# Stacking a pair of images' mixed values in 72 rows by small DMAs, one matmul per query tile in place of three masked ones

## Chip, cores and metric

The kernel runs on one core of a Trainium2 chip. The metric is the device time of one execution in microseconds (us); the median of three runs is compared. The kernel has a program for each engine: TensorE (PE; its weight loads are PEld), VectorE (DVE), ScalarE (ACT), GpSimd (POOL) and SyncE (SP), which here only issues DMAs.

## The reference

One layer of a vision tower on 128 images of 12 channels and 224x224 pixels.

```python
pooled = x.reshape(128, 12, 14, 16, 14, 16).sum(axis=(3, 5))        # 196 tokens an image
h = einsum('bcij,ce->bije', pooled, channel_weights)                # 12 -> 192
n = layernorm(h)
q, k = n[:, :64], n[:, 64:]                                         # 64 queries, 132 keys
a = softmax(q @ k.T * 12 ** -0.5 ...) @ k                           # 64 x 192 an image
a = transpose(a, (0, 2, 1)).reshape(b, 64, 192) @ proj_w.T + proj_b
h = h + concat([a, k])
h = h + moe(layernorm(h))       # 8 experts of 192-128-192 in 4 groups, 2 used a token, and a shared one
```

Only the sum over channels carries an image's content, so the kernel keeps tokens as 12 coefficients (times the fixed channel weights) as long as it can. The attention output of an image is, before the transpose, 64 queries by 12 coefficients; the transpose and reshape mix it with proj_w in three parts r = 0, 1, 2. The item "M" computes these mixed values: for each image a matrix of 12 rows (one per coefficient) and 3 x 192 columns. The query rows after attention are then, for the 64 queries i of an image, the sum over r and coefficient c of (centred channel weight of c at column 3i + r) times (mixed value of c and r), plus the token itself.

## The kernel before, in words

The images go in eight groups of 16. For each group there is an attention stage ("items": V, PHT, VHT, S, U, ET, AH, M, H, X, XT, GQ, keyG, G, gate, C) and then a feed-forward stage of 63 steps (seven chunks of tokens by nine experts). The attention stage of the next group is spread over the steps of the current one's feed-forward stage by a plan written out by hand (`PLAN`, lines 77 to 119, the items of each step); tile loads and sums of the pixels of the group after that are placed by `LATE` (line 136; `LATE0`, line 139, for the first group) in the same steps: one tile at steps 4, 6, 8, 10, 12, 13, 16, 19, 22, 25, 29 and so on, 21 tiles of 1792 KB a group through two slots. The items of the first group run ahead of the loop (lines 404, 405), beside the tile work of `LATE0`. In this document the first group is group zero of the code, the last one the eighth; "groups one to six" are those whose attention stage runs inside another's feed-forward stage with tile work beside it (second to seventh), and the last has no tile work beside it.

Each engine walks the same steps in order and waits by semaphores. On TensorE a step is: the first product of the expert (L1218 for queries, L1392 for keys), the second layer of the step before last (`layer2`, L1368 and L1370), the second product, the gate's row spread by L1397, then the plan's items. On VectorE: two elementwise products (L1123, L1133; L1120 for the shared expert), then the items' parts, then the pixel sums (L770, L777). On ScalarE: the SiLU (L732), then the pixel sums (L630), then the items' parts. On SP (`ffn_dma`, L477): at each step first the load that takes the slot of a tile just summed (`load_after`, L448), and at the fourth step of a chunk the stores of the chunk before (`store`, L468). Step 25 holds a load; step 21 holds the four stores of the second query chunk.

The item M (steps 19, 20 for the first eight images, 23, 24 for the other eight; L1290) makes the mixed values of eight images at once; ScalarE copies them to `Msb` (L681): 96 partitions (12 an image), two halves, 3 x 192 columns. The item H (eight of them, H0 to H7, steps 25 to 30, one for each 128 query rows, that is for a pair of images; L1309) adds in one PSUM bank the token part (a bf16 matmul, L1311) and three f32 matmuls (L1313), one for each r, whose moving operand is all 96 partitions of a half and whose stationary operand `CWr` is zero but for the 24 rows of the pair. VectorE then takes the bank's statistics and copies it to `h2q` (L959, L960).

```python
for q in range(3):
    last = mm(ps[:, 0:D], CWr[:, q, i % 4, :], Msb[:, i // 4, D * q:D * q + D],
              start=False, stop=(q == 2))
```

`CWr` is built once at the start: eight small DMAs (L436) put the centred weights in 8 x 12 partitions, and `spread_cwc` (L841) multiplies them eight times by a column mask made by GpSimd (L531 to L535). The small DMAs stand on SP's queue ahead of nine others (L441) and of all tile loads but the first two.

Of the kernel before, what the change touches and what calls it, by code (L numbers as in the profile page):

```python
# [118 lines left out]
}  # L119
A_FIRST = 2  # L120
# [103 lines left out]
def build(nc, x, cw, proj_w, proj_b, gate_w, gate_b, w1, w2, w3, sw1, sw2, sw3, out):  # L224
    ctx = ExitStack()
    with ctx:
# [17 lines left out]
        CWr = sb("CWr", [128, 3, 4, 128])  # L244
# [57 lines left out]
        CWr_src = Msb[0:8 * CH, 0, 0:D]  # L302
# [16 lines left out]
        rmask = gt[0:8 * CH, 0, 0:8]  # L319
# [29 lines left out]
        const_done, prep_full, prep_dve, prep_act = sem("const_done"), sem("prep_full"), sem("prep_dve"), sem("prep_act")  # L349
        cwc_ready, cwx_split, w_split, wx_in, cwx_in = sem("cwc_ready"), sem("cwx_split"), sem("w_split"), sem("wx_in"), sem("cwx_in")  # L350
# [66 lines left out]
        def _(sp):  # L417
# [16 lines left out]
            sp.wait_ge(cwc_ready, 1)  # L434
            for b in range(8):
                sp.dma_start(CWr_src[b * CH:(b + 1) * CH, :], CW14[0:CH, :]).then_inc(cwr_in, 16)  # L436
# [32 lines left out]

            def load_after(g, t):  # L470

                if t + SLOTS < TILES:
                    load(g, t + SLOTS)
                elif g.k is not None or g.off < NG - 1:
                    load(g.plus(1), t + SLOTS - TILES)

            def ffn_dma(g, left):  # L477
                for step in range(STEPS):
                    c, e = divmod(step, EX)
                    for gt_, t in tiles_at(g, step, left):  # L480
                        load_after(gt_, t)
                    if e == 3 and c > 0:
                        store(g, c - 1)
                store(g, NCH - 1)
# [3 lines left out]
            for step in range(A_FIRST, STEPS):  # L488
                for gt_, t in tiles_at(G(None, -1), step):
                    load_after(gt_, t)  # L490
            ffn_dma(G(None, 0), 2)
# [11 lines left out]
        def _(pool):  # L503
# [20 lines left out]
            for c in range(CH):  # L524
# [6 lines left out]
            link(nc.gpsimd.memset(rmask, 1.0))  # L531
            link(nc.gpsimd.affine_select(out=rmask, in_=rmask, compare_op=ALU.is_ge, fill=0.0, base=0,
                                         pattern=[[-CH, 8]], channel_multiplier=1))
            link(nc.gpsimd.affine_select(out=rmask, in_=rmask, compare_op=ALU.is_ge, fill=0.0, base=CH - 1,
                                         pattern=[[CH, 8]], channel_multiplier=-1))  # L535
# [215 lines left out]
        def _(dve):  # L751
# [35 lines left out]
            plink(v.memset(CWr[8 * CH:128, :, :, :], 0.0))  # L787
            plink(v.memset(Msb[8 * CH:128, :, :], 0.0))
# [7 lines left out]
            dve.wait_ge(pb_in, 16)  # L796
            plink(v.tensor_copy(CSP[:, 0, :], CW14[:, :]))
# [43 lines left out]
            def spread_cwc():  # L841

                dve.wait_ge(cwr_in, 16 * 8)
                for b in range(8):
                    plink(v.tensor_scalar(CWr[0:8 * CH, :, b // 2, 64 * (b % 2):64 * (b % 2) + 64],
                                          CWr_src.rearrange("p (i r) -> p r i", r=3), rmask[:, b:b + 1], None, ALU.mult))
                dve.wait_ge(cwx_in, 9 * 16)
                plink(v.memset(SPT[:, :, :, :, :].rearrange("p a b c d -> p (a b c d)"), 0.0))
                plink(v.memset(SPT[0:NQ, 0:GB, 0, 0, CH + 1:UC], 1.0))
# [299 lines left out]
        def _(pe):  # L1149
# [71 lines left out]
            def item(g, kind, i):  # L1221
# [87 lines left out]
                elif kind == "H":  # L1309

                    mm(ps[:, 0:D], UTq[:, 128 * i:128 * i + 128], CWx[:, :], start=True, stop=False)  # L1311
                    for q in range(3):
                        last = mm(ps[:, 0:D], CWr[:, q, i % 4, :], Msb[:, i // 4, D * q:D * q + D],  # L1313
                                  start=False, stop=(q == 2))
# [120 lines left out]
```

## Time and profile before

| | |
|---|---|
| median of 3 runs | 1875.4 us (1872.0 to 1878.65) |
| the profiled execution | 1880.6 us, its span 1878.9 us |
| TensorE busy | 87% of the span |
| VectorE, ScalarE, GpSimd busy | 66%, 48%, 35% |
| mean granted TensorE clock | 0.935 of full speed |
| DMA | 333 MB, 177 GB/s on average |

Everything in the profile is of one execution. Times in the timeline are microseconds from the start of the span. A group of instructions shows how often it ran, its busy time and the mean of one; an f32 matmul appears as two records. "Idle before" names what ended an engine's wait. The DMA rows give the mean busy share of the 16 DMA engines and what they moved.

### The profile page before, as it was taken

What the parts mean: (1) busy time and instruction counts of PE and PEld (TensorE: products, weight loads), DVE (VectorE), ACT (ScalarE), POOL (GpSimd) and SP (SyncE); (2) the same over time, 40 slices, a digit from 0 to 9 for tenths busy, and PEclk for the clock granted to TensorE, in tenths of its full rate; (3) what the DMA queues carried; (4) which work ended last, traced back from release to release, by engine and by line L of the source; (5) the groups of instructions that cost most, each with busy time, mean ns of one, the idle gap of its engine ahead of it and who ended that gap; (6) DMA issues with size and microseconds to landing.
All of it is one profiled execution on the core that took longest, in us unless ns stands there. A gap on an engine that the chain in (4) does not pass through costs nothing.

```text
span 1878.9 us, 31672 instructions
## 1 busy us (share of the span) xinstructions
PE 1634.6 (87%) x9665; PEld 1260.1 (67%) x9798; DVE 1239.9 (66%) x2344; ACT 905.8 (48%) x2999; POOL 657.5 (35%) x739
## 2 busy tenths in 40 slices
PE   1714639999999989998999989998999999999998
PEld 1203528866787667766787667766787678877876
DVE  6855567577666687578566677578666764566365
ACT  2324433656356654656355654656365643443132
POOL 5334326334443435334443335334534332000000
PEclk9955659989999899989999899999999999999999
DMA  8896755546554465555455455556554530000000
GB/s 304 315 352 239 289 219 196 205 165 222 205 204 182 172 222 216 180 200 207 175 205 204 168 215 204 182 198 223 195 205 174 210 131 10 10 18 18 9 19 26
DMA packets 55455, 333.14 MB, mean 177 GB/s; under 512 B 4237, under 2 KB 33666, under 8 KB 33774
## 3 DMA queue, kind: packets, MB, share of 16 engines
q1 hardware_dynamic: 55062, 330.51, 47.6%
q8 instruction: 83, 1.36, 0.3%
q14 instruction: 94, 0.77, 0.1%
q10 hardware_dynamic: 216, 0.50, 0.1%
HBM read 311.10 MB, written 19.27 MB: 176 GB/s over the span
## 4 chain that ended last, share of the span: by engine, by line
PE 69%; DVE 14%; issue 7%; DMA 6%; ACT 2%; POOL 1%; SPq 1%; DVEq 0%; ACTq 0%; another core or an unknown queue 0%; POOLq 0%
PE bank L1370 25%; PE bank L1218 19%; DMA xt<-in_x 6%; PE bank L1392 6%; PE bank L1397 3%; DVE pooled L770 2%; PE bank L1285 2%; DVE ffn L1123 2%; PE bank L1313 2%; DVE ffn L1133 2%; PE bank L1325 2%; PE bank L1274 1%; PE bank L1280 1%; PE bank L1297 1%; PE bank L1290 1%
## 5 line engine op out<-in xcount | busy, mean ns | idle before, releaser
L1370 PE MATMUL bank<-W2T,ffn 128*128 128x192 f32 (+1 forms) x3600 | 692.8, 331 | 0.0
L1370 PEld LDWEIGHTS bank<-W2T,ffn 128*128 128x128 f32 (+1 forms) x3600 | 599.7, 190 | 54.3 <-issue 6.5
L1123 DVE TENSOR_TENSOR ffn<-bank,ffn 128x512 f32<-128x512 f32 (+1 forms) x448 | 278.3, 621 | 367.7 <-PE bank L1218 161.7
L560 POOL TENSOR_TENSOR kh_sum<-xt 128x768 f32<-128x768 f32 (+2 forms) x168 | 249.1, 1483 | 738.0 <-DMA xt<-in_x 730.1
L732 ACT ACTIVATE ffn<-bank 128x512 f32<-128x512 f32 (+1 forms) x504 | 274.1, 547 | 396.0 <-PE bank L1392 211.0
L630 ACT ACTIVATE xt<-xt 128x256 f32<-128x256 f32 x776 | 312.5, 411 | 110.1 <-DMA xt<-in_x 110.1
L1133 DVE TENSOR_TENSOR ffn<-bank,ffn 128x512 f32<-128x512 f32 (+1 forms) x448 | 279.5, 624 | 40.6 <-DVE ffn L1123 33.1
L1392 PE MATMUL bank<-tokT,Wx 126*128 126x512 bf16 (+1 forms) x720 | 250.9, 353 | 25.2 <-DVE ffn L1133 12.6
L770 DVE TENSOR_REDUCE pooled<-xt 128x1 f32<-128x256 f32 (+2 forms) x168 | 233.4, 1389 | 38.9 <-DMA xt<-in_x 38.0
L555 POOL TENSOR_TENSOR kh_sum<-kh_sum 128x384 f32<-128x384 f32 (+2 forms) x336 | 230.2, 685 | 26.4
L1218 PE MATMUL bank<-x0h,WT0h 128*128 128x512 f32 x288 | 154.6, 537 | 3.0 <-issue 2.3
L630 ACT ACTIVATION_READ_ACCUMULATOR xt<-xt 128x1 f32 x776 | 151.9, 196 | 0.0
L1397 PE MATMUL bank<-cwT,sel 128*128 128x512 bf16 (+1 forms) x315 | 110.0, 349 | 27.4 <-DVE ffn L1133 27.0
L1397 PEld LDWEIGHTS bank<-cwT,sel 128*128 128x128 bf16 x448 | 43.8, 98 | 115.8 <-DVE ffn L1133 66.8
L1392 PEld LDWEIGHTS bank<-tokT,Wx 126*128 126x128 bf16 x720 | 72.0, 100 | 66.1 <-issue 21.1
L1218 PE MATMUL bank<-x1h,WT1s 128*128 128x512 f32 x288 | 114.7, 398 | 0.0
L1218 PE MATMUL bank<-x0h,WT0l 128*128 128x512 f32 x288 | 114.6, 398 | 0.0
L1218 PE MATMUL bank<-x0l,WT0h 128*128 128x512 f32 x288 | 114.3, 397 | 0.0
L1218 PE MATMUL bank<-x1l,WT1s 128*128 128x512 f32 x288 | 114.0, 396 | 0.0
L672 ACT ACT_TABLE_LOAD x28 | 35.9, 1283 | 101.5 <-PE bank L1274 51.3
L1313 PE MATMUL bank<-Msb,CWr 128*128 128x192 f32 x384 | 76.1, 339 | 0.0
L1120 DVE TENSOR_TENSOR ffn<-bank,ffn 128x512 f32<-128x512 f32 (+1 forms) x56 | 34.8, 621 | 52.2 <-ACT ffn L732 27.4
(253 smaller groups left out, 2161.8 us busy)
## 6 DMA issues: line engine op xcount, KB each, us to landing
xt<-in_x SPq DMA_DIRECT2D x168, 1792.0 KB, 7.3
out<-stage SPq DMA_DIRECT2D x192, 96.0 KB
ffn<-in_L_ffn_w SPq DMA_DIRECT2D x2, 768.0 KB
attw<-in_L_ffn_w SPq DMA_DIRECT2D x1, 512.0 KB
Wx<-tokT ACTq DMA_DIRECT2D x9, 54.2 KB
out<-stage SPq DMA_DIRECT2D x8, 48.0 KB
attw<-in_L_ffn_w SPq DMA_DIRECT2D x1, 256.0 KB
ffn<-in_L_ffn_sw SPq DMA_DIRECT2D x2, 96.0 KB
```

Source lines behind the costliest of these rows:

```text
L555: nc.gpsimd.tensor_tensor(out=out, in0=in0, in1=in1, op=ALU.add).then_inc(tree_step, 1)
L560: nc.gpsimd.tensor_tensor(out=kh, in0=src[:, 0:8, :], in1=src[:, 8:16, :], op=ALU.add).then_inc(pool_read, 1)
L630: last = nc.scalar.activation(src[:, :, j, :], src[:, :, j, :], ACT.Copy, accum_out=pooled[:, t // HALF, at:at + 1])
L732: nc.scalar.activation(silu[p][:, 0:n], h_ps(step, 0)[:, 0:n], ACT.Silu).then_inc(silu_done, 1)
L770: v.tensor_reduce(out=pooled[:, t // HALF, at + lo:at + hi], in_=src[:, lo:hi, :, :], axis=AX.XY, op=ALU.add).then_inc(dve_summed, 1)
L1123: v.tensor_tensor(out=gated[p][:, 0:n], in0=h_ps(step, 1)[:, 0:n], in1=silu[p][:, 0:n], op=ALU.mult).then_inc(gated_done, 1)
L1133: v.tensor_tensor(out=h[step % HR][:, 0:n], in0=cw_ps[:, 0:n], in1=gated[p][:, 0:n], op=ALU.mult).then_inc(h_done, 1)
L1218: ins = mm(o, left[q], right[q], start=(q == 0), stop=(q == len(left) - 1))
L1313: last = mm(ps[:, 0:D], CWr[:, q, i % 4, :], Msb[:, i // 4, D * q:D * q + D], start=False, stop=(q == 2))
L1370: last = mm(o, h[step % HR][:, 128 * t:128 * t + m], W2T[:, e, :], start=(e == 0 and query and t % 2 == 0), stop=(e == NE), skip_group_che ...
L1392: last = mm(o[:, 0:n], Wx[:, w:w + INTER], X2T[g.par][:, col:col + n], start=True, stop=True)
L1397: mm(cw_ps[:, 0:n], sel[:, e, :], cwT[:, at:at + n], start=True, stop=True).then_inc(cw_ready, 1)
```

## The change

The moving operand of H becomes a stack of 72 partitions for each pair of images (24 rows of the pair by three parts r, so that row 3p + r holds part r of row p), laid in the `h2q` tile that later takes H's own result. Four DMAs of SP for each half of a group copy it from `Msb`: the first half in step 21, after that step's stores, the second half in step 25, after that step's load (`MIX`). The stationary operand is one 72 x 128 matrix for all pairs, filled by two small DMAs from a rearranged copy that VectorE makes. TensorE waits for the half's four DMAs ahead of each H. The masks, the eight masked copies and two of the memsets go.

```diff
+MIX = {21: 0, 25: 1}
...
-        CWr = sb("CWr", [128, 3, 4, 128])
+        CWr = sb("CWr", [3 * 2 * CH, 2 * NQ])
...
-        CWr_src = Msb[0:8 * CH, 0, 0:D]
+        CWr_src = Msb[0:CH, 0, 0:D].rearrange("p (r i) -> p r i", r=3)
+
+        Mst = h2q[0:3 * 2 * CH, :, :]
...
-        rmask = gt[0:8 * CH, 0, 0:8]
...
+        cwr_ready = sem("cwr_ready")
+        mixed = [sem("mixed_first"), sem("mixed_second")]
...
-            sp.wait_ge(cwc_ready, 1)
-            for b in range(8):
-                sp.dma_start(CWr_src[b * CH:(b + 1) * CH, :], CW14[0:CH, :]).then_inc(cwr_in, 16)
+            sp.wait_ge(cwr_ready, 1)
+            for b in range(2):
+                sp.dma_start(CWr[3 * CH * b:3 * CH * (b + 1), NQ * b:NQ * b + NQ],
+                             CWr_src.rearrange("p r i -> p (r i)")).then_inc(cwr_in, 16)
...
+            def stack_mix(g, half):
+
+                sp.wait_ge(aux_act, g.at(BYACT[-1], BYACT[R[("M", 2 * half + 1)]]))
+                for m in range(4):
+                    sp.dma_start(Mst[:, 4 * half + m, :],
+                                 Msb[2 * CH * m:2 * CH * (m + 1), half, :]).then_inc(mixed[half], 16)
...
                     if e == 3 and c > 0:
                         store(g, c - 1)
+                    if left and step in MIX:
+                        stack_mix(g.plus(1), MIX[step])
...
                 for gt_, t in tiles_at(G(None, -1), step):
                     load_after(gt_, t)
+                if step in MIX:
+                    stack_mix(G(None, 0), MIX[step])
...
-            link(nc.gpsimd.memset(rmask, 1.0))
-            link(nc.gpsimd.affine_select(out=rmask, in_=rmask, compare_op=ALU.is_ge, fill=0.0, base=0,
-                                         pattern=[[-CH, 8]], channel_multiplier=1))
-            link(nc.gpsimd.affine_select(out=rmask, in_=rmask, compare_op=ALU.is_ge, fill=0.0, base=CH - 1,
-                                         pattern=[[CH, 8]], channel_multiplier=-1))
...
-            plink(v.memset(CWr[8 * CH:128, :, :, :], 0.0))
-            plink(v.memset(Msb[8 * CH:128, :, :], 0.0))
+            plink(v.memset(CWr[:, :], 0.0))
...
+            v.tensor_copy(CWr_src, CW14[0:CH, :].rearrange("p (i r) -> p r i", r=3)).then_inc(cwr_ready, 1)
...
-                dve.wait_ge(cwr_in, 16 * 8)
-                for b in range(8):
-                    plink(v.tensor_scalar(CWr[0:8 * CH, :, b // 2, 64 * (b % 2):64 * (b % 2) + 64],
-                                          CWr_src.rearrange("p (i r) -> p r i", r=3), rmask[:, b:b + 1], None, ALU.mult))
+                dve.wait_ge(cwr_in, 16 * 2)
...
+                    pe.wait_ge(mixed[i // 4], g.at(64, 64))
                     mm(ps[:, 0:D], UTq[:, 128 * i:128 * i + 128], CWx[:, :], start=True, stop=False)
-                    for q in range(3):
-                        last = mm(ps[:, 0:D], CWr[:, q, i % 4, :], Msb[:, i // 4, D * q:D * q + D],
-                                  start=False, stop=(q == 2))
+                    last = mm(ps[:, 0:D], CWr[:, :], Mst[:, i, :], start=False, stop=True)
```

## Rows read from the trace of the kernel before

**Rows 1.** The page, busy time, share and instructions of TensorE.

```profile
PE 1634.6 (87%) x9665; PEld 1260.1 (67%) x9798; DVE 1239.9 (66%) x2344; ACT 905.8 (48%) x2999; POOL 657.5 (35%) x739
```

**Rows 2.** The page, the chain that ended last, by engine and by line.

```profile
PE 69%; DVE 14%; issue 7%; DMA 6%; ACT 2%; POOL 1%; SPq 1%; DVEq 0%; ACTq 0%; another core or an unknown queue 0%; POOLq 0%
PE bank L1370 25%; PE bank L1218 19%; DMA xt<-in_x 6%; PE bank L1392 6%; PE bank L1397 3%; DVE pooled L770 2%; PE bank L1285 2%; DVE ffn L1123 2%; PE bank L1313 2%; DVE ffn L1133 2%; PE bank L1325 2%; PE bank L1274 1%; PE bank L1280 1%; PE 
```

**Rows 3.** Groups by shape: records, busy us, mean ns of one, idle before.

```profile
L1313 PE MATMUL bank<-Msb,CWr 128*128 128x192 f32 x384 | 76.1, 339 | 0.0
...
L1290 PE MATMUL bank<-projT,Asb 64*96 64x192 f32 x32 | 9.3, 373 | 0.0
```

**Rows 4.** Timeline of 0 to 60: start, us, engine line, what, count, idle before.

```profile
11.81 6.23 SPq L436 DMA_DIRECT2D Msb<-CW  x8
...
18.08 7.06 SPq L441 DMA_DIRECT2D CWx<-SPT  x9
...
18.38 2.29 DVE L770 TENSOR_REDUCE pooled<-xt 128x8 f32<-128x2048 f32 x1 [3.12 <-DMA xt<-in_x]
...
25.27 30.93 SPq L448 DMA_DIRECT2D xt<-in_x  x7
...
25.67 3.26 DVE L845 TENSOR_SCALAR CWr<-Msb,gt 96x192 f32<-96x192 f32 x8
...
32.15 2.29 DVE L770 TENSOR_REDUCE pooled<-xt 128x8 f32<-128x2048 f32 x1 [0.40 <-DMA xt<-in_x]
```

**Rows 5.** Stretches: PE, PEld, DVE, ACT, POOL busy, TensorE clock, DMA share, GB/s.

```profile
578.50:579.00 0.50, 0.50 (x12) 0.50 (x11) 0.31 (x2) 0.00 (x0) 0.00 (x0) 1.00 1.00 430
583.00:583.50 0.50, 0.50 (x3) 0.50 (x2) 0.00 (x0) 0.50 (x3) 0.50 (x1) 0.50 0.14 46
...
603.50:603.75 0.25, 0.25 (x3) 0.19 (x2) 0.00 (x0) 0.00 (x0) 0.00 (x0) 1.00 0.14 57
```

**Rows 6.** Timeline of 800 to 816, the fourth group's H: load, H0, H3, H4, SiLUs.

```profile
800.28 0.25 PE L1311 MATMUL bank<-CWx,UTq 126*128 126x192 bf16 x1
...
803.94 0.33 SPq L448 DMA_DIRECT2D xt<-in_x  x1
...
809.78 0.20 PE L1397 MATMUL bank<-cwT,sel 128*128 128x64 bf16 x1 [1.42 <-DVE ffn L1133]
809.86 0.25 PE L1311 MATMUL bank<-CWx,UTq 126*128 126x192 bf16 x1
...
810.96 0.25 PE L1311 MATMUL bank<-CWx,UTq 126*128 126x192 bf16 x1
...
812.28 0.22 ACT L732 ACTIVATE ffn<-bank 128x64 f32<-128x64 f32 x1 [2.98 <-PE bank L1392]
...
814.09 0.22 ACT L732 ACTIVATE ffn<-bank 128x64 f32<-128x64 f32 x1
```

**Rows 7.** Timeline, load of step 25 and H4 in the third and fifth groups.

```profile
597.82 0.33 SPq L448 DMA_DIRECT2D xt<-in_x  x1
...
602.67 0.25 PE L1311 MATMUL bank<-CWx,UTq 126*128 126x192 bf16 x1
...
1015.57 0.33 SPq L448 DMA_DIRECT2D xt<-in_x  x1
...
1022.66 0.25 PE L1311 MATMUL bank<-CWx,UTq 126*128 126x192 bf16 x1
```

**Rows 8.** Timeline, the first group: load of step 25, H4, and the load's landing.

```profile
212.46 0.33 SPq L448 DMA_DIRECT2D xt<-in_x  x1
...
215.55 0.25 PE L1311 MATMUL bank<-CWx,UTq 126*128 126x192 bf16 x1 [1.11 <-DVE h2q L960]
...
219.12 0.73 POOL L560 TENSOR_TENSOR kh_sum<-xt 128x256 f32<-128x256 f32 x1 [7.14 <-DMA xt<-in_x]
```

**Rows 9.** Timeline, the last group's H4 and VectorE's wait after it.

```profile
1641.96 0.25 PE L1311 MATMUL bank<-CWx,UTq 126*128 126x192 bf16 x1
...
1643.25 0.37 DVE L959 BATCH_NORM_STATS2 bst<-bank 128x6 f32<-128x192 f32 x1 [0.47 <-PE bank L1313]
```

## The prediction

> **What bounds the kernel now.** I read the busy times first. TensorE is busy 1634.6 of 1878.9 us [rows 1], so cutting its work can pay. The chain of waits agrees: TensorE carries 69% of the path, and the line that is changed, L1313, 2% of the span, some 38 us [rows 2]. That share is the reader's ceiling: 128 of the 192 matmuls of L1313 go, two thirds, so about 25 us can leave that path directly. What is left is a question of places: the item H runs eight times in each of eight image groups, always in the same steps of the plan, and I read the timeline there for what ends last.
>
> **The matmuls removed.** Busy 76.1 us over 192 matmuls (two records each) is 0.40 us each [rows 3]; back to back, one H item follows another after 1.10 us (809.86 to 810.96 [rows 6]), of which the bf16 matmul takes about 0.1, so a masked matmul holds TensorE 0.33 us and an item gets shorter by 0.67 us. If all 64 items were on the path: 64 x 0.67 = 43 us. The new matmul has 72 rows where the old ones had 96 in use of 128; no row shows 72. The 64-row matmul of the same 192 columns takes 0.373 us, the 128-row one 0.339 [rows 3], so I take 0.33 and no gain or loss by the rows.
>
> **Where a shorter H pays.** In the groups prepared under the loop (one to six), H0 to H2 pay nothing: H3 starts at 809.86 right after a matmul of L1397 that waited 1.42 us for VectorE's L1133 [rows 6], so VectorE sets the time up to there, and its own work is unchanged. From H4 to H7 TensorE is the bound, 4 x 0.67 = 2.7 us, but ScalarE comes close: in this stretch its two SiLUs are 1.81 us apart with no idle time between them (812.28 to 814.09; sums of the tile fill it) [rows 6], and no shorter TensorE step shortens that. I take 2.0 us a group, between 1.3 and 2.7. The last group has no tile loads and sums; VectorE waits 0.47 us for L1313 [rows 9] and the three early items pay partly too: 4 us, between 2.7 and 5.4.
>
> **The new wait in H4.** The second four stacking DMAs stand on SP's queue right behind the tile load of step 25. They share its queue and its engines, so they land after it. Terms, from the issue T of that load: its bytes move until T+5.8 (issued 597.82 [rows 7], the rate falls to 57 GB/s in 603.50 to 603.75 [rows 5]); the stack adds 4 x 72 rows x 768 B = 221 KB. Its own price is in no row. From above: a query store, also of 768-byte runs, moves at 46 GB/s with a DMA share of 0.14, a seventh of the engines [rows 5], 4.8 us for 221 KB. From below: at the load's 430 GB/s [rows 5] it is 0.5 us. A store's 46 GB/s on 0.14 x 16 = 2.2 engines is 20 GB/s per engine; on a dozen engines 221 KB take 0.9 us. I take 1.1 us, near the lower end, because a copy of 72 rows can be shared out while a store is cut by its two images. The landing follows the last bytes by 0.9 us (212.46 to 219.12 is 6.7 us, less 5.8 [rows 8]). Sum: T+7.8, from T+7.2 to T+11.5. The issues themselves, 0.7 to 0.8 us each as the eight of L436 took 6.23 us [rows 4], end by T+3.6, inside the load.
>
> The Trainium skill, DMA: Bandwidth & Descriptors, section on why a DMA increments its semaphore by 16, has a DMA run on the largest count up to 16 that divides the outer dimension of both sides: 2 for the query store, and 24 and 72 would give 12 here. The 0.14 of the row agrees; by that rule the stack is near my 1.1 us.
>
> H4 now starts at T+7.0 in the fourth and T+7.1 in the fifth group (803.94 to 810.96, 1015.57 to 1022.66), at T+4.9 in the third (597.82 to 602.67) [rows 6, 7]. The six groups' distances are of this kind, 38 us together by the two near 7.1 (the second group also), the short one and two near 6. T hangs on VectorE and doesn't move. So H4 starts later than before by 6 x 7.8 - 38 = 9 us in all, and the later items win back 6 x 2.0 = 12: net -3 us for six groups. With T+8.3 it would be zero.
>
> **The new wait in H0.** The first four DMAs follow the query stores of step 21. Those hold their two engines for 4 x 98 KB / 46 GB/s = 8.5 us [rows 5], and the stack's share on these engines comes behind them. In the timeline that ends 2 us or less on either side of H0's start (800.28 [rows 6]). H0 has some 0.7 us gained by its own shortening, and VectorE takes its result only after L1133, so most of it is covered. I take +1 us over all, from 0 to +8: without that cover each group would pay up to 1.4 us.
>
> **The first group** runs before the loop. Its second stack follows the load of 212.46, lands by 220.3, and H4 stood at 215.55 [rows 8]: 4.7 us late. VectorE waits there already, and each of H4 to H7 is shorter by 0.67 or more; I take +2.5, between -1 and +4.7.
>
> **Start of the run.** SP issued 8 small DMAs in 6.23 us, then 9 in 7.06, and only then the third tile's load at 25.27, though its slot was read out at 20.67 (18.38 + 2.29) [rows 4]. Now there are 2 instead of 8, 4.7 us less, so the load goes at about 20.9, 4.4 earlier. VectorE loses its 8 masked copies, 3.26 us, ahead of the sum at 32.15 that waited for the DMA [rows 4]. The tiles follow each other through two slots, so an earlier third tile moves all 18 behind it: -4 us, between -1 (if the HBM rate is already the limit) and -5. The memsets, the three GpSimd operations and the one new copy are under 1.5 us each and stand beside weight loads: nothing; were that cover gone, 1 us at most.
>
> **Clock.** A TensorE that waits can lose clock: at 583 the granted clock was 0.50 [rows 5], the 1.2 GHz level, after a stretch of tiny matmuls. Two-microsecond waits in H4 may do it again; +2 us, between 0 and +8.
>
> **Sum.** -4 + 2.5 - 3 + 1 - 4 (last group) + 2 = -5.5 us. The profiled execution took 1880.6 us (span 1878.9), 5.2 above the median of 1875.4; the difference goes on the median: 1870.
>
> **The rivals.**
> Stack in time. If the small DMAs slip past the load (other descriptors first, or issued before it), H4 doesn't wait: six groups at -2.7, the first -2, start -4, last -4, no clock loss: -26, 1849. Against it: one queue, and the load is issued first.
> Slow drain (the slower side). If the stack goes over few engines as the stores do, at four engines' rate 2.6 us and at the store's 46 GB/s 4.8 us instead of 1.1 [rows 5], seven groups wait 1.5 to 3.7 longer in H4 and about half as much in H0: +15 to +38, that is 1885 to 1908. It decides from T+9.4 on; up to there the result stays under +0.3%. For it: the only DMAs of 768-byte runs that the rates show move like that. Against: they are cut by images, the stack by rows.
> The saving is not on the path. If VectorE or ScalarE also set the time from H4 to H7, the waits cost their 9 us and win back little: about +8, 1883. For it: the SiLUs without idle time [rows 6]. Against: VectorE waits for L1313 [rows 9].
> That the change does not do what it says I leave out: the products are the same, in 72 rows.
>
> The Trainium skill, TensorE: Matmul & The Clock Gate, on loading the stationary operand, says that its time goes by columns and not by rows; by that 72 rows cost what 96 do. The 0.373 and 0.339 us of rows 3 differ the other way and leave the term as it is.
>
> **Chances.** Forecast 0.52, stack in time 0.15, slow drain 0.20, saving off the path 0.13. About 0.3% (5.6 us) is what a measurement of this kernel can tell. The forecast sits at that edge, with its own range of 1861 to 1879: half of it counts as faster, most of the rest as the same. Faster 0.43, same 0.30, slower 0.27. The range takes in the first rival and the near end of the second: 1848 to 1887.
>
> **What would show it.** In the changed profile: L1313 in 128 records and some 25 us busy; in groups one to six an idle time of TensorE before the matmul of H4, released by the DMA, 1 to 3 us, and none in the last; the stack landing 7.8 us after the load of step 25; the third tile's load near 21 us; H3 still after VectorE's L1133. I am wrong if H4 finds its semaphore set (then near 1849), if the landing is 10 us or more after T (then near 1890), if H0 waits over 2 us in most groups, or if the start doesn't move.

## The result and the profile after

The changed kernel takes 1882.1 us (median of 16 runs, 1878.7 to 1887.9) beside 1877.0 us (16 runs, 1870.8 to 1882.1) of the kernel before: ratio 1.0032, 95% interval 1.0019 to 1.0045. It is slower by 0.3%, where I had forecast 1870. Medians in this document are of all executions of a kernel, while ratios and their intervals leave out the few executions that ran in the chip's slower state. The profiled execution took 1882.5 us, its span is 1880.7.

The page of the changed kernel, busy times and the chain that ended last (as [rows 1, 2]):

```profile
PE 1632.8 (87%) x9542; PEld 1231.4 (65%) x9542; DVE 1237.1 (66%) x2336; ACT 903.8 (48%) x2999; POOL 658.2 (35%) x736
...
PE 69%; DVE 12%; DMA 7%; issue 5%; SPq 3%; ACT 3%; POOL 0%; ACTq 0%; DVEq 0%; POOLq 0%
PE bank L1377 26%; PE bank L1226 19%; PE bank L1399 6%; DMA xt<-in_x 5%; PE bank L1404 4%; DMA h2q<-Msb 3%; DVE pooled L781 2%; PE bank L1293 2%; DVE ffn L1141 2%; DVE ffn L1131 2%; SPq L479 2%; PE bank L1332 1%; PE bank L1282 1%; ACT xt L641 1%; PE bank L1314 1%
```

The masked matmuls are gone from the chain; in their place stand the stack's DMAs (3%) and their issue on SP's queue (L479, 2%). The lines have moved by 7 to 11: L1313 is L1321, L1311 is L1320, L1370 is L1377, L1392 is L1399, L1397 is L1404, L1133 is L1141. The new matmuls, by shape (as [rows 3]), and from the waits of TensorE, by whom it waited for (us in total, times, longest):

```profile
L1321 PE MATMUL bank<-h2q,CWr 72*128 72x192 f32 x128 | 46.1, 458 | 0.0
...
PE bank L1320 <- DMA h2q<-Msb: 18.2, 13, 6.2
```

One record of the new matmul takes 0.458 us in the mean, not 0.339 as in [rows 3], and the group is busy 46.1 us where I had named some 25. The rows are not the reason: in the last group, at full clock, the sixteen records of 72 rows take 0.339 us each. Much of the rest ran at half clock. And TensorE waited 13 times for the stack, 18.2 us.

Where the span went, by the starts of the groups' feed-forward stages (first L1226, before L1218):

| stretch | before | after | difference | forecast |
|---|---|---|---|---|
| start and first group | 277.6 | 279.7 | +2.1 | -1.5 |
| six groups with tile work | 1250.4 | 1254.6 | +4.3 | 0, clock included |
| last group | 350.9 | 346.3 | -4.6 | -4 |

The windows of H0 to H4, H4 to H7 and the 19 us behind them, third group, kernel before (columns: us; busy us of PE, PEld, DVE, ACT, POOL; granted clock; DMA share; GB/s):

```profile
592.56:602.67 10.11, 9.26 (x61) 8.47 (x60) 9.11 (x21) 3.73 (x15) 3.99 (x4) 1.00 0.53 199
602.67:607.33 4.66, 4.66 (x35) 3.67 (x33) 3.06 (x12) 3.23 (x16) 0.00 (x0) 1.00 0.21 88
607.33:626.30 18.97, 16.96 (x92) 9.52 (x92) 12.27 (x36) 9.34 (x39) 9.31 (x9) 0.73 0.33 119
```

and the same of the changed kernel:

```profile
596.53:607.58 11.05, 7.35 (x44) 6.09 (x45) 10.03 (x23) 3.09 (x11) 4.26 (x4) 0.87 0.84 320
607.58:612.41 4.83, 4.83 (x20) 2.86 (x21) 2.86 (x12) 3.23 (x16) 0.00 (x0) 0.50 0.02 5
612.41:631.40 18.99, 18.99 (x102) 11.16 (x101) 11.99 (x38) 10.25 (x44) 9.26 (x9) 0.66 0.38 129
```

From the start of H4 to that of H7 TensorE has three items' saving, 2.0 us, less to do and takes 0.17 us longer, since the clock is at 0.50, the 1.2 GHz level. So it is in all six groups (0.50 to 0.54, 4.57 to 4.83 us; before 1.00 and 4.66). What led up to it, TensorE's timeline of the same group:

```profile
602.48 0.19 PE L1399 MATMUL bank<-tokT,Wx 126*128 126x64 bf16 x1
605.99 0.23 PE L1404 MATMUL bank<-cwT,sel 128*128 128x64 bf16 x1 [3.31 <-DVE ffn L1141]
606.18 0.32 PE L1320 MATMUL bank<-CWx,UTq 126*128 126x192 bf16 x1
606.29 0.90 PE L1321 MATMUL bank<-h2q,CWr 72*128 72x192 f32 x2
607.58 0.32 PE L1320 MATMUL bank<-CWx,UTq 126*128 126x192 bf16 x1 [0.39 <-DMA h2q<-Msb]
607.69 0.90 PE L1321 MATMUL bank<-h2q,CWr 72*128 72x192 f32 x2
```

TensorE idles 3.31 us for VectorE ahead of H3 (0.85 us in this group before; over the six groups 16.0 us for 5.5), which no term of mine had, and what follows runs at half speed: 0.90 us for the pair of records where 0.52 is its time at full clock.

What VectorE did meanwhile, and GpSimd beside it, changed kernel:

```profile
601.14 2.21 DVE L889 TENSOR_TENSOR SPT<-res,SPT 98x384 bf16<-98x384 f32 x1
603.39 2.00 DVE L892 COPY SPT<-SPT 98x1344 bf16<-98x1344 bf16 x2
...
601.13 1.80 POOL L571 TENSOR_TENSOR kh_sum<-xt 128x768 f32<-128x768 f32 x1 [10.04 <-DMA xt<-in_x]
603.02 2.00 POOL L566 TENSOR_TENSOR kh_sum<-kh_sum 128x384 f32<-128x384 f32 x2
```

and before:

```profile
599.36 0.56 DVE L881 TENSOR_TENSOR SPT<-res,SPT 98x384 bf16<-98x384 f32 x1
599.96 0.93 DVE L884 COPY SPT<-SPT 98x1344 bf16<-98x1344 bf16 x2
...
594.89 1.81 POOL L560 TENSOR_TENSOR kh_sum<-xt 128x768 f32<-128x768 f32 x1 [8.70 <-DMA xt<-in_x]
596.77 1.87 POOL L555 TENSOR_TENSOR kh_sum<-kh_sum 128x384 f32<-128x384 f32 x2
```

The two pieces of VectorE, unchanged in the code, take 4.21 us instead of 1.49, as GpSimd sums a tile at the same time. In the kernel before the two came to 2.63 us in five groups (a part of the sum overlapped) and 1.49 in one; in the changed kernel to 3.77 or more in all six. So the two engines met in most groups already, and meet for longer now. GpSimd starts when its tile lands, and that tile's load, of step 22, now stands behind the first stack on SP's queue. SP in the fourth group, changed kernel:

```profile
788.87 8.95 SPq L473 DMA_DIRECT2D out<-stage  x4
797.93 4.49 SPq L479 DMA_DIRECT2D h2q<-Msb  x4
802.77 0.35 SPq L453 DMA_DIRECT2D xt<-in_x  x1
```

The load goes 2.5 us before H0 (805.28); before it went at 796.05, 4.2 us before H0 (800.28). All six groups show it: 4.2 to 4.7 us ahead of H0 then, 2.3 to 2.8 now.

The Trainium skill, GPSIMD Engine Reference, section on specifications, says that GpSimd's SBUF interfaces are shared with VectorE, with contention for VectorE's instructions with two SBUF inputs or in a two-port mode. The trace agrees for L889, which has two such inputs: 0.56 us alone (kernel before), 2.21 beside GpSimd.

### The profile page after: what moved, and what is told of

It reads as the page before. It is cut to its first block, busy times and chain, and to the rows that moved or that the text cites. A ratio compares the mean times of both kernels' runs of the same rounds, so it can differ in the third digit from the quotient of the medians.

```text
span 1880.7 us, 31387 instructions
## 1 busy us (share of the span) xinstructions
PE 1632.8 (87%) x9542; PEld 1231.4 (65%) x9542; DVE 1237.1 (66%) x2336; ACT 903.8 (48%) x2999; POOL 658.2 (35%) x736
## 3 DMA queue, kind: packets, MB, share of 16 engines
q1 hardware_dynamic: 60342, 333.99, 48.2%
## 4 chain that ended last, share of the span: by engine, by line
PE 69%; DVE 12%; DMA 7%; issue 5%; SPq 3%; ACT 3%; POOL 0%; ACTq 0%; DVEq 0%; POOLq 0%
PE bank L1377 26%; PE bank L1226 19%; PE bank L1399 6%; DMA xt<-in_x 5%; PE bank L1404 4%; DMA h2q<-Msb 3%; DVE pooled L781 2%; PE bank L1293 2%; DVE ffn L1141 2%; DVE ffn L1131 2%; SPq L479 2%; PE bank L1332 1%; PE bank L1282 1%; ACT xt L641 1%; PE bank L1314 1%
## 5 line engine op out<-in xcount | busy, mean ns | idle before, releaser
L1377 PE MATMUL bank<-W2T,ffn 128*128 128x192 f32 (+1 forms) x3600 | 702.6, 334 | 0.0
L1377 PEld LDWEIGHTS bank<-W2T,ffn 128*128 128x128 f32 (+1 forms) x3600 | 600.3, 190 | 57.4 <-issue 8.6
L1141 DVE TENSOR_TENSOR ffn<-bank,ffn 128x512 f32<-128x512 f32 (+1 forms) x448 | 279.5, 624 | 40.7 <-DVE ffn L1131 33.0
L1399 PE MATMUL bank<-tokT,Wx 126*128 126x512 bf16 (+1 forms) x720 | 252.6, 356 | 0.0
L1404 PE MATMUL bank<-cwT,sel 128*128 128x512 bf16 (+1 forms) x448 | 163.6, 365 | 51.1 <-DVE ffn L1141 50.6
L1226 PE MATMUL bank<-x0h,WT0h 128*128 128x512 f32 x288 | 154.7, 537 | 2.7 <-issue 2.0
L1404 PEld LDWEIGHTS bank<-cwT,sel 128*128 128x128 bf16 x448 | 44.3, 99 | 128.7 <-DVE ffn L1141 80.7
L1399 PEld LDWEIGHTS bank<-tokT,Wx 126*128 126x128 bf16 x720 | 74.7, 104 | 63.2 <-ACT ffn L743 29.3
L1226 PE MATMUL bank<-x0h,WT0l 128*128 128x512 f32 x288 | 114.8, 399 | 0.0
L1226 PE MATMUL bank<-x1h,WT1s 128*128 128x512 f32 x288 | 114.8, 399 | 0.0
L1226 PE MATMUL bank<-x0l,WT0h 128*128 128x512 f32 x288 | 114.6, 398 | 0.0
L1226 PE MATMUL bank<-x1l,WT1s 128*128 128x512 f32 x288 | 114.0, 396 | 0.0
L706 ACT CAST tokT<-bank 126x256 bf16<-126x256 f32 x128 | 49.0, 383 | 41.2 <-PE bank L1314 41.2
```

Of the source, the lines that this page charges most:

```text
L706: nc.scalar.copy(dst[:, 0:2048].rearrange("p (c b k) -> p b c k", c=4, b=GB)[:, 2 * i:2 * i + 2, :, :], src[:, :, 0:128].rearrange("p b (c ...
L1141: v.tensor_tensor(out=h[step % HR][:, 0:n], in0=cw_ps[:, 0:n], in1=gated[p][:, 0:n], op=ALU.mult).then_inc(h_done, 1)
L1226: ins = mm(o, left[q], right[q], start=(q == 0), stop=(q == len(left) - 1))
L1377: last = mm(o, h[step % HR][:, 128 * t:128 * t + m], W2T[:, e, :], start=(e == 0 and query and t % 2 == 0), stop=(e == NE), skip_group_che ...
L1399: last = mm(o[:, 0:n], Wx[:, w:w + INTER], X2T[g.par][:, col:col + n], start=True, stop=True)
L1404: mm(cw_ps[:, 0:n], sel[:, e, :], cwT[:, at:at + n], start=True, stop=True).then_inc(cw_ready, 1)
```

## The experiments

Sixteen runs, in the order in which they were made. "Early" and "late" tell where the stack's DMAs stand. The last column counts, of the six groups in the profiled execution, those whose clock was 1.00 from H4 to H7; run 2's profiled execution was the slowest of its nine and isn't read.

| run | stack | H items | other | us, median | ratio (95%) | clock held |
|---|---|---|---|---|---|---|
| changed kernel | late | light | | 1882.1 | 1.0032 (1.0019-1.0045) | 0 |
| 1 | both early | light | | 1865.3 | 0.9920 (0.9888-0.9951) | 1 |
| 2 | second early | light | | 1866.8 | 0.9916 (0.9885-0.9947) | |
| 3 | none | light | mixed values not stacked | 1865.6 | 0.9935 (0.9913-0.9956) | 1 |
| 4 | late | all filled | | 1916.0 | 1.0202 (1.0169-1.0234) | 1 |
| 5 | both early | all filled | | 1881.8 | 1.0047 (1.0020-1.0075) | 5 |
| 6 | both early | H0-H2 filled | | 1849.2 | 0.9869 (0.9841-0.9897) | 5 |
| 7 | both early | light | six more DMAs at the start | 1865.8 | 0.9950 (0.9929-0.9972) | 0 |
| 8 | both early | light | as 1 | 1861.8 | 0.9928 (0.9897-0.9958) | 2 |
| 9 | late | H0-H2 filled | | 1885.9 | 1.0035 (1.0017-1.0053) | 0 |
| 10 | both early | H0-H2 filled in six groups | | 1858.2 | 0.9888 (0.9864-0.9912) | 3 |
| 11 | both early | H0-H2 filled | as 6 | 1852.0 | 0.9867 (0.9841-0.9893) | 5 |
| 12 | both early | H0-H2 half filled | | 1856.6 | 0.9882 (0.9858-0.9906) | 3 |
| 13 | both early | light | GpSimd's sum later | 1835.7 | 0.9770 (0.9750-0.9790) | 6 |
| 14 | late | light | GpSimd's sum later | 1880.9 | 1.0023 (1.0005-1.0042) | 0 |
| 15 | (before) | three masked | GpSimd's sum later | 1864.9 | 0.9934 (0.9911-0.9956) | 6 |
| 16 | both early | H0-H2 filled | GpSimd's sum later | 1843.4 | 0.9810 (0.9791-0.9829) | 6 |

### Runs 1 to 4: is it the wait, or the lighter items?

Two theories: W, the waits for the DMAs took the gain; C, the lighter items leave TensorE idle behind VectorE and cost the clock, the waits only add a little.

Run 1, both stacks ahead of the stores and of the load, in the first group's loop too; run 2 has `MIX[step] == 1` alone:

```diff
+                    first = step in MIX and (MIX[step] == 0 or MIX[step] == 1)
+                    if left and first:
+                        stack_mix(g.plus(1), MIX[step])
                     for gt_, t in tiles_at(g, step, left):
                         load_after(gt_, t)
                     if e == 3 and c > 0:
                         store(g, c - 1)
-                    if left and step in MIX:
+                    if left and step in MIX and not first:
```

> Edit: SP issues each half's four stacking DMAs ahead of what stands before them now (the first half ahead of the stores of step 21, the second ahead of the load of step 25). The matmuls are the changed kernel's. Theory W, that the waits of H0 and H4 for the stack took the gain: both waits vanish in groups one to six, H4 to H7 run at full clock, and the time is 15 to 25 us under the kernel before (ratio 0.987 to 0.992). Theory C, that the lighter steps leave TensorE idle behind VectorE in steps 26 to 28, the granted clock falls there to 0.5 and the wait only adds to it: the waits vanish too, but the clock of H4 to H7 stays at 0.5 to 0.7 in most groups and the time is within 6 us of the kernel before (ratio 0.997 to 1.003).

> Edit: only the second half's four stacking DMAs are issued ahead of the load of step 25; the first half stays behind the stores. Theory W: H4's wait is gone (it was 1 to 2 us of idle and the longer half of the loss), H0's of 0.6 to 1.6 us stays, the time is some 10 us under the changed kernel (ratio to before 0.994 to 0.999). Theory C: under 5 us against the changed kernel (ratio 0.999 to 1.004), the clock in H4 to H7 still at 0.5 to 0.7.

Run 3, no stacking DMAs and no wait. H reads the first 72 rows of `Msb`, so it leaves out applying the mixed values as the reference does:

```diff
-                    pe.wait_ge(mixed[i // 4], g.at(64, 64))
-                    last = mm(ps[:, 0:D], CWr[:, :], Mst[:, i, :], start=False, stop=True)
+                    last = mm(ps[:, 0:D], CWr[:, :], Msb[0:3 * 2 * CH, i // 4, 0:D], start=False, stop=True)
```

> Edit: no stacking DMAs and no wait for them; H's one f32 matmul reads the first 72 rows and first 192 columns of the mixed values of its half, so the mixed values are not applied as in the reference. This is the removal of the 128 matmuls (and the shorter start) by itself. Theory W: 20 to 30 us under the kernel before (ratio 0.984 to 0.990), clock in H4 to H7 1.00. Theory C: the removal alone leaves TensorE idle for 2 us and more in step 27 or 28 and the clock falls in H4 to H7 in most of groups one to six; gain 5 us from the last group and 2 from the start, and at most 5 from the other six (ratio 0.993 to 0.998).

Run 4, the old amount of matmuls, two of them with zero weights:

```diff
+                    for q in range(2):
+                        mm(ps[:, 0:D], CWz[:, :], Mst[:, i, :], start=False, stop=False)
                     last = mm(ps[:, 0:D], CWr[:, :], Mst[:, i, :], start=False, stop=True)
```

> Edit: the changed kernel with two more f32 matmuls of the same form in each H, on a stationary operand of zeros, so that TensorE has the work of the kernel before and the result stays. Theory W: the filling costs what the removal gained, 10 to 25 us over the changed kernel (ratio to before 1.008 to 1.016). Theory C: the clock stays at 1.00 more often between H0 and H7 (mean of the run 0.925 to 0.935 where the changed kernel had 0.913) and the time is within 5 us of the changed kernel (ratio to before 1.000 to 1.006).

Runs 1 to 3 came out together, 15 to 17 us below the changed kernel. So the wait of H4, the first group's included, is worth about that, and H0's wait is worth nothing that shows (run 2 keeps it). Nor does the stack's traffic show a cost (run 3 has none). The ranges are split: run 1 came out in W's, run 3 in C's, and run 2 below both. And W had the runs without a wait at full clock, which they were not: run 1, third group, wait ahead of H3 and window H4 to H7:

```profile
602.94 0.20 PE L1410 MATMUL bank<-cwT,sel 128*128 128x64 bf16 x1 [2.59 <-DVE ffn L1147]
...
603.76:608.63 4.87, 4.87 (x21) 2.91 (x20) 3.40 (x13) 3.23 (x16) 0.00 (x0) 0.50 0.03 8
```

One group of six held it, with 2.72 us from H4 to H7. Run 4 fell outside both: 34 us above the changed kernel, 16 of them between H4 and H7 in the six groups (44.8 us for 28.7), where the fillers ran at half clock in five. So C was right that light items without a wait lose the clock, and wrong about the price of the wait and about run 4, where filling alone did not bring the clock back.

### Runs 5 to 8: fill without a wait; the start

Run 5 is run 1 with run 4's filling (all eight items); run 6 fills only H0 to H2 (`range(2 if i < 3 else 0)`); run 8 repeats run 1. Run 7 is run 1 with

```diff
+            for b in range(2, 8):
+                sp.dma_start(Msb[b * CH:(b + 1) * CH, 0, 0:D], CW14[0:CH, :]).then_inc(cwr_in, 16)
```

behind the two DMAs that fill `CWr`, and VectorE waits for all eight.

> Both halves' stacks go ahead of the stores and the load, and each H item has two more f32 matmuls with zero weights, so TensorE has the old amount of work and no DMA to wait for. Until now: lighter without wait left H4 to H7 at clock 0.50 in most groups, and the old amount with the wait too (1.0202 of before). Theory D (either is enough: the wait or the lighter items lose the clock): here neither is left, so H4 to H7 take 4.66 us at clock 1.00 as in the kernel before, and the time is that of before less a little at the start: ratio 0.996 to 1.001, 1869 to 1879 us. Rival P (the clock goes for another reason that the change brings, the place of the items against the small DMAs or against VectorE): the filled H4 to H7 run at 0.50 to 0.55 as in the filled run with the wait, 7.6 to 8.7 us each, six groups of 3 to 4 us more: ratio 1.009 to 1.014, 1893 to 1903 us.

> As the run before, but only H0, H1 and H2 of each group have the two zero-weight matmuls; H3 to H7 have one. Theory D1 (what decides the clock of H4 to H7 is how much TensorE has to do in steps 25 to 27, where VectorE sets the time anyway): filling costs nothing there, the clock of H4 to H7 is 1.00, they take 2.7 us instead of 4.9, and each of the six groups is 3 to 5 us shorter than with both halves early alone (1865.3 us, ratio 0.992), as the one group of that run whose clock held was (204.0 us against 207 to 208): 1838 to 1850 us, ratio 0.980 to 0.987. Rival D2 (the idle time just before H3 and the short items from H3 on decide): the clock stays 0.50 in most groups, and the filled items cost nothing or at most 0.7 us a group: 1864 to 1871 us, ratio 0.992 to 0.996.

> Both halves early, and at the start of the run six more small DMAs behind the two that fill CWr (to rows that nobody reads), so that SP issues eight there as in the kernel before; the eight masked copies of VectorE stay out. Told against the same kernel without them in this job. Theory F (the forecast's term: the third tile's load hangs on SP's queue and moves all tiles behind it): third tile's load about 4.7 us later, the first group starts 3 to 5 us later, 1868 to 1870.5 us where the other takes 1865.3. Rival G (the first group's loads are spaced by the summing, so the lead is lost on the way; the changed kernel's first group came only 1.7 us nearer where its third tile had come 3.5 nearer): 0.5 to 2 us later, 1866 to 1867.5 us.

> The same kernel as the first of both halves early (1865.3 us, ratio 0.992), again, beside the others on one chip, as what they are told against. Theories D, D1, F and G alike: 1863 to 1868 us, ratio 0.989 to 0.995; how many of the six groups keep the clock in H4 to H7 (one of six before) may differ by one.

Run 6 is the first clear step: 12.6 to 16.1 us less than runs 8 and 1 by the medians, 10 to 11 by the ratios, by adding matmuls that compute nothing. They stand where TensorE waits for VectorE anyway, and the clock holds in five groups of six. That bears out D1. Run 5's profile agrees with D (five groups at 1.00, H4 to H7 in 4.66 us), but its median, 1881.8, lies above D's range of 1869 to 1879; the profiled execution, 1874.6, was one of its fastest, so the others may have lost more. Why the filled items lose it more easily than the old ones is open.

Run 7 against run 8, SP's timeline, run 7 and then run 8:

```profile
25.68 0.92 SPq L455 DMA_DIRECT2D xt<-in_x  x2
```

```profile
20.81 4.62 SPq L453 DMA_DIRECT2D xt<-in_x  x2
```

The third tile's load goes 4.9 us later and the medians lie 4.1 apart, but their ratios' intervals overlap, and run 7's 1865.8 lies just under G's range, since run 8 came out 3.5 below run 1, its like, and 1.2 below its own range. The first group's feed-forward stage starts at 278.7 in run 7, and at 275.4, 276.5 and 277.6 in the profiles of runs 8, 1 and 13, whose code is the same up to there: 1.1 to 3.3 us later. Neither F, my own term (3 to 5), nor G (0.5 to 2) is settled by that.

### Runs 9 to 12: does the wait lose the clock by itself; how much filling

Run 9 is the changed kernel with run 6's filling. Run 10 is run 6 without filling in the first and last group, run 11 repeats run 6, run 12 has one filler instead of two.

> The changed kernel with its DMAs where they are (waits in H0 and H4), and only H0, H1 and H2 with the two zero-weight matmuls. What is open: whether the wait of H4 loses the clock by itself. Theory D (the waits or the light items, either is enough): H4 to H7 run at clock 0.50 in most groups, and the time is that of the changed kernel within 4 us, ratio 1.001 to 1.005. Rival E (the light items H0 to H2 alone lose the clock, the waits cost only their own microseconds): H4 to H7 at clock 1.00 and 2.7 us, each of six groups about 4 us shorter than in the changed kernel: ratio 0.990 to 0.995, 1857 to 1866 us.

> Both halves early and H0 to H2 filled, as in the run of 1849.16 us (ratio 0.9869), but in the six groups with tile work only, neither in the first group nor in the last. In the last group VectorE's share is small: 3 items of 0.67 us come back there, at most 2 us (its part was 189.1 us filled and 187.8 not); in the first group TensorE runs at clock 0.50 anyway and waits for VectorE, so 0 to 1 us. Expected by both theories of the clock (the amount of work in H0 to H2 of the group itself decides): 1846 to 1849 us, ratio 0.984 to 0.987, clock of H4 to H7 1.00 in five or six of six groups. If what is filled in one group carried over to the next, the first of the six groups would lose its clock: 4 us more.

> The kernel of 1849.16 us (ratio 0.9869) again, as what the others of this job are told against: 1847 to 1852 us, ratio 0.984 to 0.989, whatever the theory.

> Both halves early, and one zero-weight matmul instead of two in H0, H1 and H2. If the clock answers to the work of H0 to H2 by degrees, three or so of the six groups hold it and the time lies half way between none (1861.8 and 1865.3 us) and two (1849.2): 1854 to 1858 us, ratio 0.989 to 0.992. If one is enough: 1847 to 1851 us, ratio 0.984 to 0.988. If it needs both: 1861 to 1866 us, ratio 0.992 to 0.996.

Run 9 is 34 to 37 us above runs 11 and 6, which differ from it only by the place of the DMAs: its clock from H4 to H7 is 0.50 to 0.70 in every group. So the wait loses the clock even with H0 to H2 filled, and then costs double what it does among light items. Run 12 held three groups and lies between, as "by degrees" had it. Run 10 missed its range by 9 us with three groups held, though its six groups have the same code as run 11's. The number held thus varies between kernels that do the same there, and something that varies had to be found.

### Runs 13 to 16: GpSimd's sum beside VectorE's copies

Over the traces of runs 1, 3, 7 and 8 (light items, no wait) there are 24 groups. In four the clock held; in these the two pieces of VectorE took 1.49 us together. In the other twenty they took 2.62 to 4.15 us, and the clock was 0.50 to 0.55. Run 3 shows that the stack is not needed for this: without it the pieces take 2.62 or 2.63 us in five groups, as in the kernel before, and 1.49 in one, and the clock goes in those five. So GpSimd's sum of the tile of step 29 was made to wait for the copies:

```diff
             def step_pool(g, step, left):
                 for gt_, t in tiles_at(g, step, left):
+                    if step == 29 and (g.k is not None or g.off >= 0):
+                        pool.wait_ge(x_rep, g.plus(1).at(2, 2))
```

> Both halves early, no filling, and GpSimd's pixel sum of the tile of step 29 waits until VectorE's copies of step 26 are done. Theory K (that sum, beside the copies, makes them two to three times longer, TensorE waits for VectorE ahead of H3, and the light H0 to H2 make that wait long enough to lose the clock): the copies take 1.49 us in all six groups, the wait ahead of H3 is about 1 us, H4 to H7 run at clock 1.00 in five or six groups and take 2.7 us, and each group is 5 to 8 us shorter than where the clock was lost: 1838 to 1850 us, ratio 0.980 to 0.986. Rival (the collision is only a companion; something else in the light items loses the clock): copies short, clock still 0.50 in most groups, 1857 to 1865 us, ratio 0.990 to 0.995.

> The changed kernel, stacks where they are, with GpSimd's sum made to wait in the same way. Theory K: the 2.3 us by which the copies are longer in every group go, but the wait for the second stack takes the place of most of it, since its landing hangs on the load of step 25 and not on VectorE: TensorE idles for the DMA instead, the clock of H4 to H7 is 0.5 to 0.7, and the time is 1872 to 1882 us, ratio 0.997 to 1.003. Rival (the collision alone made the change slow, the DMA waits are harmless): clock 1.00 and 1845 to 1860 us, ratio 0.983 to 0.991.

> The kernel before with GpSimd's sum made to wait in the same way: the control. There the copies took 2.63 us in five of six groups and 1.49 in one, TensorE waited 0.2 to 1.6 us ahead of H3, and the clock held. Theory K: the copies fall to 1.49 us, which gives at most 1.1 us in five groups; clock unchanged: 1868 to 1876 us, ratio 0.996 to 1.000. Rival (GpSimd's wait by itself speeds up or slows down the tile stream): outside of 0.994 to 1.002.

> Early stacks, H0 to H2 filled (1849.2 and 1852.0 us before), and GpSimd's sum made to wait. Theory K: with the copies short the filling has nothing left to save; it costs what it did in the last group (1.3 to 2.9 us) and a little where H0 to H2 now reach the path: 1842 to 1850 us, equal to the unfilled kernel of this job within 4 us, ratio 0.981 to 0.986. Rival (filling and collision are independent): it is 5 us or more faster than the unfilled one.

Run 13, fourth group: TensorE ahead of H3, VectorE, GpSimd, and the windows of H0 to H4, H4 to H7 and after:

```profile
794.46 0.20 PE L1412 MATMUL bank<-cwT,sel 128*128 128x64 bf16 x1 [1.05 <-DVE ffn L1149]
...
792.33 0.56 DVE L897 TENSOR_TENSOR SPT<-res,SPT 98x384 bf16<-98x384 f32 x1
792.92 0.93 DVE L900 COPY SPT<-SPT 98x1344 bf16<-98x1344 bf16 x2
...
794.07 1.81 POOL L577 TENSOR_TENSOR kh_sum<-xt 128x768 f32<-128x768 f32 x1 [11.72 <-DVE SPT L900]
...
787.27:795.08 7.81, 6.76 (x45) 5.92 (x44) 7.21 (x20) 3.75 (x15) 1.01 (x1) 1.00 0.71 247
795.08:797.80 2.72, 2.72 (x22) 1.76 (x20) 2.36 (x10) 2.05 (x11) 2.48 (x4) 1.00 0.66 275
797.80:816.80 19.00, 16.74 (x108) 10.36 (x107) 14.05 (x42) 12.11 (x56) 9.56 (x10) 0.91 0.42 141
```

All six groups look like this: copies 1.49 us, a wait of 0.76 to 1.23 us, H4 to H7 in 2.70 to 2.73 us at full clock, and a clock of 0.91 in the 19 us behind, where the groups that lost it in run 8 had 0.62 to 0.71. The time, 1835.7 us, is even under K's range, and this version beats the kernel before by 2.3% (ratio 0.977) and the changed one by 46 us. Run 16 says that the filling has nothing left to save and costs 7.7 us, about twice what K allowed between the two. Run 15, the control, is 12.5 us below its own kernel before, outside K's range and just inside the rival's: TensorE's wait ahead of H3 vanished in all six groups. So GpSimd's collision was a cost of the kernel before too, and a larger one than the 1.1 us of copy time a group that I saw in it. The cast ahead of the two pieces (L880 before) had been stretched as well, to 1.51 to 1.57 us in three groups, for 0.35 in run 15 (L882 there); fourth group, kernel before:

```profile
804.44 1.81 POOL L560 TENSOR_TENSOR kh_sum<-xt 128x768 f32<-128x768 f32 x1 [8.90 <-DMA xt<-in_x]
804.95 1.52 DVE L880 CAST SPT<-res 98x384 bf16<-98x384 f32 x1
```

From H0 to H3 the six groups take 6.8 us less (47.7 for 54.5), and the 19 us behind H7 have a clock of 0.82 or 0.91 where four groups had 0.73. Whether the wait of GpSimd also moves the tile stream, as the rival has it, run 15 leaves open; run 14, with the same wait and no gain, shows that it brings little by itself.

Run 14, the fourth group, has short copies, and a wait for the stack in their place:

```profile
812.82 0.32 PE L1322 MATMUL bank<-CWx,UTq 126*128 126x192 bf16 x1 [3.48 <-DMA h2q<-Msb]
...
812.82:817.65 4.83, 4.83 (x21) 2.86 (x21) 2.58 (x10) 3.23 (x16) 0.00 (x0) 0.50 0.01 3
```

Six such waits of 3.48 to 4.67 us, and 1880.9 us, as K had it. Undoing the wait alone gave 17 to 20 us (runs 1, 8), the collision alone 1 us (run 14), both 46 us (run 13). With the light items in place, each of the two is enough to lose the clock.

## Why the prediction was wrong, point by point

**What failed** is the term "I take 2.0 us a group", the 12 us that H4 to H7 were to win back, together with "Clock ... I take +2 us". I had the two beside each other and priced the clock as if the gain were safe from it. But the gain needs the light items at full clock, and at half clock they take 4.57 to 4.83 us from the start of H4 to that of H7, as much as the old ones: measured +0.8 us over six groups from H4 to H7 (28.7 for 27.9) where I had -12. The 19 us behind went from a clock of 0.73 to 0.91 to one of 0.64 to 0.68. The row at 583 from which I priced the clock [rows 5] is of a TensorE that had been busy for 4.8 of the 5 us before, 32 matmuls of 12 columns among them; the +2 us had no row of a wait behind it. That the last group, where nothing of this happens, gave 4.6 us shows the direct saving sized right.

**"H0 to H2 pay nothing ... VectorE's own work is unchanged"** was right as to time and missed its other side. Three items 0.67 us shorter, in front of an engine that is waited for, are 2.0 us more idle time in one place; [rows 6] showed the 1.42 us that were there already. Three groups of run 1 and five of run 3 show that this is enough by itself: no wait for the stack, the two pieces as long as in the kernel before (2.62 or 2.63 us), and the clock lost behind 2.12 to 3.21 us of waiting for VectorE. The second part was wrong in the trace: the same instructions took up to 2.7 us longer, by GpSimd's sum.

**The issues of the first stack** I costed by H0's wait alone, and only the second's as time on the queue. The load of step 22 behind them went about 1.9 us later against H0, and GpSimd's sum, which starts at its landing, then lay upon more of VectorE's copies in every group. That the one made the other is read from the traces; no run moved this load alone. The waits in H0 were 0.6 to 1.6 us (5.3 in all), close to the "up to 1.4 us" each, and on the path they cost nothing that run 2 could show.

**The landing** was right: T+7.8, measured 7.7 to 7.9 in five of the six groups' loads and the first group's, 9.0 in one. "Slow drain", the rival on the slower side, is refuted by that: the result has its sign, by another mechanism. H4 stood 48.2 us behind the issue of its load in the six groups together, for 38.0 before: 10.2 us later, forecast 9. TensorE's own waits in it came to 6.8 us; their price came by the clock. That 1882 lies in the wider range of 1848 to 1887 is luck: it was drawn for other mechanisms.

**The first group**: 6.2 us of wait where I had 4.7, first group's timeline, changed kernel:

```profile
217.31 0.32 PE L1320 MATMUL bank<-CWx,UTq 126*128 126x192 bf16 x1 [6.18 <-DMA h2q<-Msb]
```

**The start**: third tile's load at 20.98, forecast 20.9; run 7 gives the term 1.1 to 3.3 us by the profiles, forecast 4. The stretch as a whole came out at +2.1 for -1.5: with the stack early (runs 8, 1, 13) the first feed-forward stage starts at 275.4, 276.5 and 277.6 instead of 279.7, so the first group's wait cost 2.1 to 4.3 us net, inside its range (up to 4.7) and around the 2.5 I took. Each figure is of one execution.

**The rivals.** "Stack in time", 1849, is what runs 1 and 8 set up: 1862 to 1865, because the clock is lost without a wait too. Once GpSimd is out of the way the rival is right in size: run 13 is 29 us below run 15, its like with three masked matmuls, where the rival had 26. "The saving is not on the path" gave 1883 and is nearest to the result, but its reason is refuted: in run 13 H4 to H7 take 2.7 us for 4.66, the whole 2.0 us of three items.

The Trainium skill, TensorE: Matmul & The Clock Gate, section on how oscillation bites in real kernels, tells of short bursts of matmuls with DMA waits between them that start each burst at half clock. Run 14 against run 13 agrees (waits of 3.48 to 4.67 us, then 0.50 to 0.56). In run 1 a wait for an engine did the same: 2.59 us for VectorE ahead of a clock of 0.50.

What stays open is run 5's median, and why a wait of about the same length lost the clock in one group and not in another (within run 12, held after 2.69 us for VectorE and lost after 2.12).

## What to carry to other kernels

Before work is taken from an engine, look for what it waits for next: time saved ahead of a wait on another engine is idle time in one piece, and if TensorE's clock falls in it, the matmuls behind, where the saving was to be had, pay it back. Small DMAs on a queue of large loads cost twice, by landing behind the load ahead of them and by holding up the load behind them, and a load that moves takes other engines' work along (read from the traces here, not tested by itself); move such an engine's work out of the way before judging the change. Where one disturbance masks another, undoing each alone shows little: try them together.

## What the hardware showed that was not expected

A bf16 copy of VectorE of 98 x 1344 (two instructions) takes 0.93 us alone and 1.39 to 3.29 us where GpSimd's sums run beside it for a part or all of the time. Adding f32 matmuls with zero weights ahead of a wait made the kernel 10 to 16 us faster (run 6 beside runs 1 and 8), and adding the same to the items behind the wait made it 33 us slower again (run 5 beside run 6). A kernel whose clock hangs on such a wait scatters: 1846.7 to 1873.0 us over 11 executions of run 8, with mean clocks of 0.927 and 0.911, while run 13 stayed within 1831.3 to 1837.5.
